# Attention's output product and the first network's down product in three fp32r passes each, with the low part of the outputs made by VectorE

## What is computed

```python
# first attention: 16 heads of 128, causal; latent c_kv of 128
q = (x @ wq).reshape(B, T, H, Dh)
c_kv = x @ w_down
kv_up = (c_kv @ w_up).reshape(B, T, H, 2 * Dh)
k, v = (kv_up[..., :Dh], kv_up[..., Dh:])
...                                          # rope on q and k, causal softmax
out = jnp.einsum('bhqk,bkhd->bqhd', attn, v).reshape(B, T, H * Dh)
return out @ wo
# first network, per token: a gated product with low-rank experts (rank 8, top 2 of 8)
# hidden of 688; down: hidden @ W_down plus the experts' (hidden @ A_down) @ B_down
```

## Time and profile before

| | us |
|---|---|
| runs | 1445.7, 1446.26, 1450.47 (median 1446.26) |
| profiled execution | 1456.95, its span 1455.1 |
| granted clock, mean | 0.986 |
| attention's steps | about 38 to 630 of the span |
| first network | about 638 to 821 |
| output product, one step (8 instructions) | 1.73 |
| down product, one batch (48 instructions) | 13.29 |

### The profile page before, as it was taken

How to read it: one execution, slowest core, us unless ns; L and a number is a source line. 1 busy time by engine, 2 the same in 40 slices (tenths; PEclk the granted TensorE clock), 3 DMA queues, 4 the chain that set the end, 5 groups by cost and what they waited for, 6 DMA issues and landing times.

```text
span 1455.1 us, 23920 instructions
## 1 busy us (share of the span) xinstructions
PE 1383.6 (95%) x7940; PEld 1107.0 (76%) x7940; DVE 947.3 (65%) x2442; ACT 578.6 (40%) x1455; POOL 550.7 (38%) x480
## 2 busy tenths in 40 slices
PE   8999999999999999899999999999999999986995
PEld 7777777777777777577777788788788788863564
DVE  4787877777777777773453467567557557893226
ACT  4444444444445444542122243333343333441232
POOL 3655555555555555301014023513523512204122
PEclk9999999999999999999999999999999999997998
DMA  6000000000002000120000020110010001686994
GB/s 184 1 12 1 12 0 11 0 11 0 11 0 73 1 0 1 22 66 1 0 1 1 10 72 8 35 53 9 24 63 7 15 8 40 167 277 208 285 269 134
DMA packets 67951, 76.14 MB, mean 52 GB/s; under 512 B 14189, under 2 KB 55173, under 8 KB 67877
## 3 DMA queue, kind: packets, MB, share of 16 engines
q1 hardware_dynamic: 56533, 58.36, 13.9%
q10 hardware_dynamic: 8560, 12.36, 2.9%
q0 software_dynamic: 2784, 4.46, 1.5%
HBM read 66.22 MB, written 8.95 MB: 52 GB/s over the span
## 4 chain that ended last, share of the span: by engine, by line
PE 77%; DVE 9%; POOL 4%; ACT 3%; issue 3%; DMA 2%; another core or an unknown queue 1%; SPq 1%; POOLq 0%; DVEq 0%; ACTq 0%
PE ps L1762 38%; PE ps L1902 9%; PE ps L1876 7%; PE ps L1863 5%; PE ps L1937 4%; PE ps L2028 4%; PE ps L1869 2%; PE ps L2111 2%; DMA wo<-in_L_attn_wo_dram 1%; PE ps L2101 1%; PE ps L2338 1%; PE ps L2260 1%; DVE pT_low L1123 1%; PE ps L2320 1%
## 5 line engine op out<-in xcount | busy, mean ns | idle before, releaser
L827 ACT ACTIVATE probs<-ps,nm 128x128 f32<-128x128 f32 (+3 forms) x256 | 134.2, 526 | 171.7 <-DVE nm L1211 171.6
L664 POOL TENSOR_TENSOR qk<-q,ksb 128x512 f32<-128x512 f32 x64 | 83.4, 1303 | 283.6 <-ACT q L922 211.2
L1123 DVE TENSOR_TENSOR pT_low<-ps,pT 128x384 fp32r<-128x384 f32 (+2 forms) x256 | 99.6, 451 | 114.6 <-ACT pT L753 113.4
L1902 PE MATMUL ps<-kT,qT 128*128 128x128 f32 (+3 forms) x512 | 162.0, 439 | 8.7 <-ACT probs L827 8.6
L1140 DVE TENSOR_TENSOR prod<-ps,rope_sb 128x1024 f32<-128x1024 f32 x128 | 150.6, 1219 | 7.4 <-PE ps L1762 7.4
L538 POOL TENSOR_TENSOR qT<-prod 64x512 f32<-64x512 f32 x64 | 81.1, 1267 | 158.3 <-DVE prod L1140 153.5
L753 ACT ACTIVATE pT<-ps 128x384 fp32r<-128x384 f32 (+2 forms) x256 | 84.8, 417 | 122.5 <-PE ps L1937 122.5
L1876 PEld LDWEIGHTS ps<-U,oT 128*128 128x128 f32 x512 | 98.1, 192 | 41.0 <-issue 19.7
L1211 DVE CUSTOM_DVE_ANT_0 ps<-ps,causal 128x128 f32<-128x128 f32 (+3 forms) x256 | 120.8, 511 | 11.3 <-PE ps L1902 10.5
L1876 PE MATMUL ps<-U,oT 128*128 (+1 forms) x512 | 122.0, 381 | 0.0
L538 POOL TENSOR_TENSOR kT<-prod 64x512 f32<-64x512 f32 x64 | 81.4, 1273 | 99.9 <-DVE prod L1140 97.5
(11 more groups left out here) (283 smaller groups left out, 2765.8 us busy)
## 6 DMA issues: line engine op xcount, KB each, us to landing
eg<-in_L_ffn_w_gate_dram SPq DMA_DIRECT2D x16, 704.0 KB
eg<-in_L_ffn_w_up_dram SPq DMA_DIRECT2D x16, 704.0 KB
ed<-in_L_ffn_w_down_dram ACTq DMA_DIRECT2D x10, 640.0 KB
ksb<-ks_dram SPq DMA_DIRECT2D x16, 256.0 KB, 3.3
ed<-in_L_ffn_w_down_dram SPq DMA_DIRECT2D x6, 640.0 KB
rows_dram<-rows ACTq DMA_DIRECT2D x4, 640.0 KB, 8.7
acc<-in_L_attn_x_dram SPq DMA_DIRECT2D x4, 512.0 KB
wq_in<-in_L_attn_wq_dram SPq DMA_DIRECT2D x8, 256.0 KB, 2.9
```

The lines of the kernel that those rows point to most:

```text
L664: nc.gpsimd.tensor_tensor(qk[:], q3[:], ksb[b % 2][:], ALU.mult).then_inc(qk_ready, 1)
L827: nc.scalar.activation(probs[hh][:, off:off + (i + 1) * P], ps[:, BS + i % 2, 0:(i + 1) * P], ACT.Exp, bias=nm[:, hh, i:i + 1], scale=-1.0 ...
L1123: return nc.vector.tensor_tensor(o, whole, hi.bitcast(F32), ALU.subtract)
L1902: pe.matmul(ps[:, bank, 0:(i + 1) * P], qT[:, hh, b, i * P:(i + 1) * P], kT[:, hh, b, 0:(i + 1) * P], start=True, stop=True).then_inc(scor ...
```

## The change

U is split: ScalarE copies each pair of heads to U_high (at 174 KB), GpSimd subtracts and writes U_low over U itself, the first pair of heads' parts before step 0, the others one in each of the first pair's steps. ScalarE's copy of BO becomes oT_high (fp32r); VectorE subtracts it from BO into oT_low (`o_rest`), between its two rope products (in the last pair's late steps, where there are none, after maximum 1; after the last step, behind `route0`). The output product is eight passes with oT_high (U_high, U_low for each of four tiles), then a wait for oT_low, then four passes with U_high.

The down product's operands are split likewise: hid_high by ScalarE after each hidden tile and ahead of its next SiLU, hid_low by VectorE in place, one tile late; dn_high and dn_low in the first batch. The down product is 12 passes with hid_high and 6 with hid_low for each token tile.

To make room, gu_in moves to 89 KB, over U's first heads, and its load and dn's wait until pair 5 has used them; dn moves to 174 KB; ldn's two loads come after the last addition; the first sigmoid waits for VectorE's rest of lb; wo, pT_low and the second layer's first key weights shift by 1 to 6 KB.

```diff
+        U_low = place("U_low", 89, [P, HEADS, D], F32R)
+        U_high = place("U_high", 174, [P, HEADS, D], F32R)
...
-            sp.wait_ge(u_ready, 8)
+            sp.wait_ge(out_ready, 2 * STEPS * (PAIRS - 2))
...
+            def u_rest(j, turned):
+                pool.wait_ge(roped, 4 * turned)
+                pool.wait_ge(uhi_ready, uhi_first + j + 1)
+                nc.gpsimd.tensor_tensor(U_low[:, 2 * j:2 * j + 2, :], U[:, 2 * j:2 * j + 2, :],
+                                        U_high[:, 2 * j:2 * j + 2, :].bitcast(F32), ALU.subtract).then_inc(ulo_ready, 1)
...
-                    copy(oT[:], ps[:, BO, :]).then_inc(ot_copied, 1)
+                    copy(oT_high[:], ps[:, BO, :]).then_inc(ot_copied, 1)
...
+                if first and n < HEADS // 2 - 1:
+                    u_high(n + 1)
...
             def scores0(b):
                 act.wait_ge(logits_ready, b + 1)
+                if b == 0:
+                    act.wait_ge(w0_lo, w0_first + 6)
...
                     nc.scalar.activation(gated[m % 2][0:size, :], ps[0:size, m % 2, :], ACT.Silu).then_inc(gated_ready, 1)
+                    act.wait_ge(hid_ready, b * FT0 + (m + 1))
+                    copy(hid_high[m // 2][0:size, m % 2, :], hidT[0:size, m, :]).then_inc(hidhi_ready, 1)
+                    if b == 0 and m in (1, 2):
+                        dn_halves(m - 1)
...
+            def o_rest(s):
+                dve.wait_ge(ot_copied, s + 1)
+                rest(oT_low[:], ps[:, BO, :], oT_high[:]).then_inc(olo_ready, 1)
...
                 for w in range(2):
+                    if w and between is not None:
+                        o_rest(between)
...
+                    if m:
+                        hid_rest(b, m - 1)
+                    if b == 0 and m in (2, 3):
+                        dn_rest(m - 2)
...
             take_weights()
+            o_rest(STEPS * PAIRS - 1)
             add(STEPS * PAIRS - 1, STEPS - 1)
...
-                    pe.wait_ge(ot_copied, s)
+                    pe.wait_ge(olo_ready, olo_first + s)
...
-                    last = pe.matmul(ps[:, BW + i // 2, (i % 2) * D:(i % 2 + 1) * D], oT[:, i * P:(i + 1) * P],
-                                     U[:, bass.ds(2 * g + n % 2, 1), :], start=True, stop=True)
+                    for part in (U_high, U_low):
+                        pe.matmul(ps[:, BW + i // 2, (i % 2) * D:(i % 2 + 1) * D], oT_high[:, i * P:(i + 1) * P],
+                                  part[:, bass.ds(2 * g + n % 2, 1), :], start=i % 2 == 0 and part is U_high, stop=False,
+                                  skip_group_check=True)
+                pe.wait_ge(olo_ready, olo_first + s + 1)
+                for i in range(TPB):
+                    last = pe.matmul(ps[:, BW + i // 2, (i % 2) * D:(i % 2 + 1) * D], oT_low[:, i * P:(i + 1) * P],
+                                     U_high[:, bass.ds(2 * g + n % 2, 1), :], start=False, stop=True,
+                                     skip_group_check=True)
```

More of the change, by code:

```diff
@@ L108, in program @@
         wvT = place("wvT", 191, [P, HEADS, DH])
-        wo = place("wo", 173, [P, HEADS, D])
+        wo = place("wo", 174, [P, HEADS, D])
         identr = place("identr", 207, [P, P], F32R)
@@ L113, in program @@
         pT = place("pT", 164, [P, TPB - 1, T], F32R)
[L114 removed]
+        pT_low = place("pT_low", 191, [P, TPB - 1, T], F32R)
         pT_end = place("pT_end", 207, [P, P])
[L116 to L119 removed]
+        oT_high = place("oT_high", 172, [P, T], F32R)
+        oT_low = place("oT_low", 197, [P, T], F32R)
+        gu_in = place("gu_in", 89, [P, KD, 2, F0])
         lb_in = place("lb_in", 137, [NL, 2, F0])
[L121 removed]
+        dn = place("dn", 174, [M0, FT0, D + NL])
         la_in = place("la_in", 143, [P, KD, NA])
[L123 removed]
+        dn_low = place("dn_low", 191, [M0, FT0, D + NL], F32R)
+        dn_high = [place(f"dn_high{j}", at, [M0, FT0 // 2, D + NL], F32R) for j, at in enumerate((198.6875, 150))]
+        ldn = place("ldn", 140, [NL, D])
         gu = [place(f"gu{h}", 20 + 11 * h, [P, KD, 2, F0], F32R) for h in range(2)]
@@ L131, in program @@
         hidT = place("hidT", 76, [M0, FT0, T])
+        hid_low = place("hid_low", 76, [M0, FT0, T], F32R)
+        hid_high = [place(f"hid_high{j}", at, [M0, 2, T], F32R) for j, at in enumerate((170, 186, 154))]
         haT = place("haT", 88, [NL, T])
@@ L889, in x2_rows, with dn_halves @@
                 copy(x2[0][:, t, 0:D - 1], acc[:, t, 0:D - 1]).then_inc(x2hi_ready, 1)
+            def dn_halves(j):
+                act.wait_ge(dn_loaded, 13 * 16)
+                if j:
+                    act.wait_ge(acc_added, 4 * STEPS * PAIRS)
+                if j == 0:
+                    copy(dn_high[0][:], dn[:, 0:3, :]).then_inc(dn_hi, 1)
+                else:
+                    copy(dn_high[1][:, 0:1, :], dn[:, 3:4, :])
+                    copy(dn_high[1][0:114, 1:3, :], dn[0:114, 4:6, :]).then_inc(dn_hi, 1)
             def ffn0(b, last):
@@ L1132, in split_wk, with products @@
                 rest(wk[1][:], wk_in[:], wk[0][:]).then_inc(wk_lo, 1)
-            def products(idx, parity, early):
+            def o_rest(s):
+                dve.wait_ge(ot_copied, s + 1)
+                rest(oT_low[:], ps[:, BO, :], oT_high[:]).then_inc(olo_ready, 1)
+            def products(idx, parity, early, between=None):
                 dve.wait_ge(proj_ready, idx + 1)
@@ L1216, in step @@
                 if n <= STEPS - LOOK or not last:
-                    products(s + (LOOK - 1), (n + 1) % 2, False)
+                    products(s + (LOOK - 1), (n + 1) % 2, False, None if first and n == 0 else s - 1)
+                else:
+                    o_rest(s - 1)
                 top(2)
@@ L1912, in step @@
                 scores(3)
+                if first and n == 1:
+                    pe.wait_ge(ulo_ready, ulo_first + 1)
                 if not (first and n == 0):
@@ L2021, in ffn0 @@
                     turn_x2(1, 4)
-                pe.wait_ge(hid_ready, b * FT0 + FT0)
+                if first:
+                    pe.wait_ge(dn_loaded, 13 * 16)
+                    pe.wait_ge(dn_lo, dn_first + 2)
+                pe.wait_ge(hidhi_ready, hidhi_first + b * FT0 + FT0)
                 for i in range(TPB):
@@ L2026, in ffn0 @@
                         turn_x2(2, 4)
+                    t = slice(i * P, (i + 1) * P)
                     for m, (f, size) in enumerate(F0S):
-                        last = pe.matmul(ps[:, i, 0:D + NL], hidT[0:size, m, i * P:(i + 1) * P], dn[0:size, m, :],
-                                         start=m == 0, stop=m == FT0 - 1)
+                        rows_in = hid_high[m // 2][0:size, m % 2, t]
+                        pe.matmul(ps[:, i, 0:D + NL], rows_in, dn_high[m // 3][0:size, m % 3, :], start=m == 0, stop=False)
+                        pe.matmul(ps[:, i, 0:D + NL], rows_in, dn_low[0:size, m, :], start=False, stop=False)
+                    if i == 0:
+                        pe.wait_ge(hidlo_ready, hidlo_first + b * FT0 + FT0)
+                    for m, (f, size) in enumerate(F0S):
+                        last = pe.matmul(ps[:, i, 0:D + NL], hid_low[0:size, m, t], dn_high[m // 3][0:size, m % 3, :],
+                                         start=False, stop=m == FT0 - 1)
                     last.then_inc(down_ready, 1)
```

42 lines of the change are left out of this document (32 added, 10 removed).

## The result

The changed kernel takes 1452.18 us (median of 12 runs), the kernel before on the same chip 1446.89: ratio 1.0036, 95% interval 1.0027 to 1.0046. It is slower by some 5 us. I had forecast 1441.2 with a range up to 1450; sign and range were both wrong.

What follows compares the result with a forecast made beforehand. TensorE was taken to bound attention and network, with VectorE nearly the bound in attention. Terms -1.5 + 0.4 + 0.6 + 2.9 - 9.9 + 2.4 = -5.1 us took 1446.26 to 1441.2, range 1431 to 1450.

Steps and rivals of the forecast that it cites:

- Part 1: Attention's output product on TensorE: twelve fp32r passes replace four fp32 matmuls, 0.29 us less a step, 18.6 over 64 steps.
- Part 2: VectorE's added rest between rope products: short steps 8.65 us, long 9.53, a pair gains only 0.06; -1.5 us taken.
- rival A: Attention: VectorE has cover after all, so both gains arrive, -22.2 us, 1424; short steps of 8.13 its sign; chance 0.11.
- Rival B: Attention: VectorE's loop costs more than counted, 1450 to 1453 us; long steps that don't shrink its sign; chance 0.15.
- once per pair of heads the rest of wk sits in the same chain and takes some of it: Attention steps: this rest uses up some of the 1.7 us gained over 28 pairs of steps; -1.5 taken with another wait.
- Rival D: Second network: GpSimd's weight halvings block the hidden tiles' rests, 0.6 in each of three batches, +1.8 us, 1443; chance 0.06.
- The other high parts of U and GpSimd's rests ... nothing on the path: First pair of heads: one more instruction a step on ScalarE and GpSimd, engines with low busy times, costs nothing.
- Part 3: Last pair of heads: the rest falls between maxima, three steps lose 0.1 to 0.4 us and gain nothing, +0.6.
- the moved loads, put at nothing: Gate and up weights' load and the two ldn loads, moved later, keep enough time before their first reader: no cost.
- Part 4: Hand-over from attention to network: the low part's rest stands behind routing and delays the last passes, +2.9 us.
- rival C: Hand-over: TensorE's pause of about 2.9 us halves its clock, costing 1.7 us, 1443; chance 0.22.
- Part 5: Network's down product: 288 passes replace 192 instructions, -9.9 us; stalls from copies and rests of hidden tiles, +2.4.

Runs made afterwards that it cites:

- run 9: Changed kernel without the rest of the outputs (no oT_low; third pass takes oT_high, low part left out): ratio 0.9875 to the kernel before.
- run 7: Changed kernel with GpSimd's last rope sum of each pair's third step waiting for VectorE's rest of wq: ratio 1.0012 to the kernel before.
- run 4: Changed kernel with the last part of U_low (ScalarE's copy and GpSimd's rest) made one step earlier: ratio 1.0005 to the kernel before.
- run 2: Changed kernel with one part undone: down product alone kept, ratio 0.9948 to the kernel before; attention part alone kept, 1.0082.
- run 5: Changed kernel without the first sigmoid's wait for VectorE's rest of lb, its tiles placed elsewhere: ratio 1.0028 to the kernel before.

## Why the prediction was wrong

**Part 1 (passes)** was right: starts 0.12 apart, and run 9 shows the full gain once nothing else holds the step.

**Part 2 (VectorE's chain)** had the mechanism and nearly the size. A short step with the long one after it lasts 18.11 against the forecast 18.18 and 18.24 before. TensorE stalls 0.33 ahead of the last four transposes, named by the additions; I had said 0.52. Against run 9 the whole loss is 0.47 a pair. The single steps came out otherwise than I wrote: 8.11 for the short one (forecast 8.65) and 10.00 for the long one (9.53). A step is measured between its first transposes, and the stall stands behind the first of them, so it falls into the next interval; I had booked it one step too early. For this reason neither the short steps of 8.1, which I had named as a sign of rival A, nor the long ones that didn't shrink, the sign of B, decide anything here; the pair does. What failed is the next sentence, "once per pair of heads the rest of wk sits in the same chain and takes some of it". There it was the rest of wq, and it didn't take some: +0.75 us in each of seven pairs, 5 us, where all pairs of steps together had gained 28 x 0.13 = 3.6. Run 7 gives 0.64 of the 0.75 to GpSimd. I costed that step by the length of the chain and didn't ask what GpSimd does beside it once it is shifted by 0.9 us.

**Rival D** was that mechanism, in the wrong place. I looked for it at the hidden tiles' rests and excused the attention, since its new rest reads PSUM. The new rest does escape (681 to 693 ns in all 64), and at the hidden tiles only one rest of 24, in the last batch, was hit (1.31 us at 798.51, with GpSimd busy from 796.88 to 799.27). But the new rest delayed the second rope product, with it GpSimd's sums, and so pushed them onto an old instruction with both inputs in SBUF. A second case stands in the first pair of heads, where GpSimd's U_low and VectorE's rest of wk start together:

```profile
84.00 1.55 DVE L1173 TENSOR_TENSOR wk<-wk_in,wk 128x256 fp32r<-128x256 f32 x1
```

```profile
83.98 1.29 POOL L564 TENSOR_TENSOR U_low<-U,U_high 128x512 fp32r<-128x512 f32 x1
```

It takes 0.41 otherwise. In both cases VectorE ends 0.13 us sooner after GpSimd's end than its own length (0.55 of 0.68, 0.28 of 0.41): it stands still for nearly the whole time that the two run side by side (0.63 of 0.76 us, 1.14 of 1.27). The Trainium skill, "SBUF - State Buffer" (two separate sides), says that whichever of the two starts first holds the shared port for its whole instruction and the other blocks. The trace agrees: 1.31 and 1.55 us instead of 0.68 and 0.41, with GpSimd's instruction the first to start in both, and run 7 shows the cause for the first of them.

**"The other high parts of U and GpSimd's rests ... nothing on the path"** is the step that failed outright: put at nothing, it cost 5.2 us (run 4), 3.67 of them the wait for the last of U_low, the remainder a slower clock behind it. I compared busy shares, 278 of 535 us for GpSimd, and didn't look at who waits for the last of the eight rests. The loop's entry is a single wait for all of them.

**Part 3**, +0.6, came out as -1.9, but not by its reason. 1.7 us of it is the step that the kernel before ran at a granted clock of 0.86 in its second profile; at full clock the difference is -0.2. Inside that, the fourth and the fifth step (T59 to T61) grew by more than I had given all of the last pair, from 8.10 and 7.94 us to 8.79 and 8.68, and a wait for a DMA on the path that I hadn't counted got 1.0 us shorter (2.31 to 1.32), which the moved loads, put at nothing, may explain (run 2).

**Part 4 (hand-over)**: the pause before the third pass was right (3.15 us forecast "about 3"), the sum not: 6.1 for 2.9. I had the sigmoid's new wait cost 0.3, by VectorE's time alone; it cost 2.0 (run 5). Behind it stood the table load, 1.28 us, which the earlier trace rows don't show since they are VectorE's and TensorE's. The clock after the pause, rival C, came true as well: 0.57 for four microseconds. I had given C a time within my range and not added it to a slower hand-over.

**Part 5** was right: 10.84 us a batch (677.33 to 680.04 is one token tile of four, below) where I had 10.8, and what is left of the stretch is 2.3 us where I had 2.4 of stalls.

```profile
677.33 0.90 PE ps L2125 x6
...
680.04 0.90 PE ps L2125 x6
```

**Rival B**, slower, was given 0.15 as one mechanism: a VectorE loop above 1.15 us. Its time, 1450 to 1453, is what was measured, but by coincidence and not by its reason: the loop's steady part came out better than my forecast. The 1.1 us lost behind the first network are not settled; stretches behind the keys differ by as much between kernels that are the same there (492.0 to 494.4), where TensorE's pauses in routing and its clock fall differently.

## What to carry to other kernels

An added instruction moves everything behind it on its engine, and through the semaphores the work of engines that it never names: ask for every shifted engine what now runs beside it, and ask it of the old instructions too. A wait placed ahead of an activation holds back its table load as well. And where one instruction is to be squeezed into a full loop, try its places: behind the next product instead of ahead of it, the same rest cost 0.13 us a pair of steps instead of 0.47. Last, a stretch that gets faster or slower between two profiles may owe it to the granted clock: read the clock of each step before naming a cause.

## What the runs showed of the hardware

- A VectorE instruction with both inputs in SBUF takes 1.31 us instead of 0.68 beside a GpSimd one that reads SBUF, 1.55 instead of 0.41 in the worst case seen, and 0.68 again when the two are kept apart by a semaphore (680 to 682 ns in eight).
- The same pause of TensorE doesn't always bring the same clock: after 1.93 us of idle time one step took 10.65 us at a granted clock of 1.00 in one execution and 12.33 at 0.86 in another; after 3.66 or 3.67 us a step took 15.30 at 0.89, 16.06 and 16.50 at 0.79.
- The expert stage of the same program takes 117 to 120 us on two chips and 108 to 109 on a third, each in a session of its own, which makes some 10 us of 1450. Kernels are compared by ratios on one chip; times between chips are not comparable.
